# A selective-scan layer on one core: ScalarE's carry copy between the two halves of a step's exponentials

## The reference

```python
dA  = exp(dt_t[:, :, None] * A)                       # A = -exp(A_log), (512, 64)
hst = hst * dA + (dt_t * x_t)[:, :, None] * B_t[:, None, :]
y_t = einsum('bds,bs->bd', hst, C_t)                  # for every t, in order
```

## Time and profile before

| what | value |
|---|---|
| time, median of 3 runs | 5366.41 us (5361.21 to 5369.36) |
| the profiled execution | 5370.79 us |
| its span, first to last instruction | 5369.1 us |
| TensorE, VectorE busy | 93%, 88% of the span |
| GpSimd, ScalarE busy | 70%, 64% |
| mean granted TensorE clock | 0.987 of full speed |

### The profile page before, as it was taken

The page is one execution under the profiler, slowest core; times in us unless marked ns, Lnnn a source line. Parts: engine busy times, 40 slices in busy tenths (PEclk is TensorE's granted clock), DMA queues, the critical chain, the costliest instruction groups (busy, mean ns, idle before and its releaser), DMA issues. The chain is left out here.

```text
span 5369.1 us, 130492 instructions
## 1 busy us (share of the span) xinstructions
PE 4970.5 (93%) x44784; PEld 2522.5 (47%) x44784; DVE 4726.2 (88%) x2419; ACT 3415.8 (64%) x11498; POOL 3751.7 (70%) x6613
## 2 busy tenths in 40 slices
PE   6999999999999999999999999999999999886898
PEld 4444444444444444444444444444444444443444
DVE  2999999999999999999999999999999999996443
ACT  4666766666666766666676766666676766663112
POOL 4777768677777868777776868677776868674211
PEclk8999999999999999999999999999999999998899
DMA  3121111111121111112121111111121211113441
GB/s 106 38 64 43 54 48 52 54 39 61 38 64 42 55 48 52 55 38 61 38 64 43 61 41 52 55 37 61 39 63 39 64 38 43 36 29 104 146 153 66
DMA packets 433144, 306.75 MB, mean 57 GB/s; under 512 B 215920, under 2 KB 336240, under 8 KB 432496
## 3 DMA queue, kind: packets, MB, share of 16 engines
q1 hardware_dynamic: 428272, 294.39, 18.2%
q10 hardware_dynamic: 4224, 4.19, 0.2%
HBM read 187.27 MB, written 111.15 MB: 56 GB/s over the span
## 5 line engine op out<-in xcount | busy, mean ns | idle before, releaser
L891 DVE TENSOR_TENSOR_SCAN b_hs<-b_dA,b_u 128x1024 f32<-128x1024 f32 x2048 | 4540.7, 2270 | 273.9 <-ACT b_u L818 187.0
L1056 PE MATMUL b_ex<-b_dd,b_aw 32*128 32x512 f32 x8192 | 2710.1, 642 | 33.7 <-POOL b_dd L534 15.4
L1043 PE MATMUL b_u<-b_ud,b_bw 32*128 32x256 f32 x16384 | 2336.5, 401 | 258.9 <-DVE b_hs L891 237.6
L800 ACT ACTIVATE b_dA<-b_ex 128x496 f32<-128x496 f32 x4096 | 2289.7, 589 | 145.4 <-PE b_ex L1056 142.6
L1043 PEld LDWEIGHTS b_u<-b_ud,b_bw 32*128 32x128 f32 x16384 | 1425.9, 184 | 1119.1 <-issue 635.5
L1075 PE MATMUL b_y<-b_hs,b_cw 128*32 128x256 f32 x16384 | 1309.9, 390 | 2.3 <-DVE b_hs L891 2.3
L818 ACT ACTIVATE b_u<-b_hin 128x32 f32<-128x32 f32 x1792 | 364.7, 203 | 1192.2 <-PE b_u L1043 1006.9
L534 POOL TENSOR_TENSOR b_dd<-b_dr,b_mask 128x512 f32<-128x512 f32 x1024 | 1073.2, 1048 | 52.2 <-DVE b_hs L891 39.4
L543 POOL TENSOR_TENSOR b_ud<-b_ur,b_mask 128x512 f32<-128x512 f32 x1024 | 1083.5, 1058 | 0.0
L1056 PEld LDWEIGHTS b_ex<-b_dd,b_aw 32*128 32x128 f32 x8192 | 856.6, 183 | 106.7 <-ACT b_dA L800 65.9
L570 POOL TENSOR_TENSOR b_hm<-b_first,b_hs 128x32 f32<-128x32 f32 x1792 | 480.1, 268 | 539.4 <-ACT b_first L799 517.8
(11 more groups left out here) (104 smaller groups left out, 2283.1 us busy)
## 6 DMA issues: line engine op xcount, KB each, us to landing
b_u<-scratch_ut SPq DMA_DIRECT2D x256, 128.0 KB, 2.9
scratch_y<-b_ysb SPq DMA_DIRECT2D x128, 256.0 KB, 2.3
scratch_xs<-b_xs SPq DMA_DIRECT2D x64, 256.0 KB, 2.4
scratch_sz<-b_sd SPq DMA_DIRECT2D x64, 256.0 KB, 2.2
scratch_dt<-b_sd SPq DMA_DIRECT2D x64, 256.0 KB, 2.1
scratch_ut<-b_uT SPq DMA_DIRECT2D x64, 256.0 KB, 2.4
b_ur<-scratch_ut SPq DMA_DIRECT2D x1024, 16.0 KB
b_dr<-scratch_dt SPq DMA_DIRECT2D x1024, 16.0 KB, 1.7
```

The source lines that it names most:

```text
L800: nc.scalar.activation(dA[:, j % NDA, h, :, 1:TC], src[:, :, 1:TC], ACT.Exp).then_inc(exp_done, 1)
L891: nc.vector.tensor_tensor_scan(hs[:, v, :, :, kp].rearrange("p d t -> p (d t)"), dA[:, j % NDA, :, :, :].rearrange("p h d t -> p (h d t)") ...
L1043: ins = nc.tensor.matmul(dst[:, :, tb, :], bw[row(r), c % 2, tb, :], ud[row(r), j // 2 % NPR, tb, :, :], start=(tb == 0), stop=(tb == NTB ...
L1056: nc.tensor.matmul(e[bank_of[what]][:, :], aw[row(r), p % DIRS, v, :, :].rearrange("p b s -> p (b s)"), dd[row(r), (p * PAIRS + j // 2) % ...
```

## The change

In `one_pass` of ScalarE, the two halves of `decay` are called apart: half 0 of step j+2 ahead of `put_carry(p, j)`, half 1 behind it. `decay` gets the half as an argument; its waits for `scanned` and `hin_made` go with half 0, the wait for `e_done` stays with each half. The order in ScalarE's queue was carry copy, L799 and L800 of half 0, L799 and L800 of half 1; it becomes L799 and L800 of half 0, carry copy, L799 and L800 of half 1. Nothing is changed on the other engines.

```diff
-                def decay(p, j):
+                def decay(p, j, h):
                     c, k, kp, v = place(j)
-                    act.wait_ge(scanned, scanned_to(p, j - NDA))
+                    if h == 0:
+                        act.wait_ge(scanned, scanned_to(p, j - NDA))
+                        if c:
+                            act.wait_ge(hin_made, hin_to(p, j - NM))
+                    src = e[bank_of["e", 2 * (p * JP + j) + h]][:, :].rearrange("p (d t) -> p d t", t=TC)
+                    act.wait_ge(e_done[2 * (1 - kp) + h], p * (JP // 2) + (j // 2 + 1))
                     if c:
-                        act.wait_ge(hin_made, hin_to(p, j - NM))
-                    for h in range(2):
-                        src = e[bank_of["e", 2 * (p * JP + j) + h]][:, :].rearrange("p (d t) -> p d t", t=TC)
-                        act.wait_ge(e_done[2 * (1 - kp) + h], p * (JP // 2) + (j // 2 + 1))
-                        if c:
-                            nc.scalar.activation(e0[:, j % NM, h, :], src[:, :, 0], ACT.Exp).then_inc(e0_done, 1)
-                        nc.scalar.activation(dA[:, j % NDA, h, :, 1:TC], src[:, :, 1:TC], ACT.Exp).then_inc(exp_done, 1)
+                        nc.scalar.activation(e0[:, j % NM, h, :], src[:, :, 0], ACT.Exp).then_inc(e0_done, 1)
+                    nc.scalar.activation(dA[:, j % NDA, h, :, 1:TC], src[:, :, 1:TC], ACT.Exp).then_inc(exp_done, 1)
...
                     for j in range(JP):
                         half = (p * JP + j) // HALF
+                        then = (p, j + 2) if j + 2 < JP else None if last else (p + 1, j + 2 - JP)
+                        if then:
+                            decay(*then, 0)
                         if j >= STEPS:
                             put_carry(p, j)
-                        if j + 2 < JP:
-                            decay(p, j + 2)
-                        elif not last:
-                            decay(p + 1, j + 2 - JP)
+                        if then:
+                            decay(*then, 1)
...
-                decay(0, 0)
-                decay(0, 1)
+                for j in range(2):
+                    for h in range(2):
+                        decay(0, j, h)
```

## The result

| kernel | median, us | runs | ratio to before, 95% |
|---|---|---|---|
| before | 5366.5 (5361.2 to 5369.4) | 4 | |
| changed | 5484.4 (5481.1 to 5492.0) | 4 | 1.0223 [1.0205, 1.0241] |

A forecast was written before the change was run, and what follows sets the result against it. It took VectorE's scans (busy 4726.2 of 5369.1 us) and their loop through injection and carry copy as the bound; 140 us for back-to-back steps plus 10 for steps with a gap gave +150, 5516 us, range 5440 to 5600.

The forecast's parts named there:

- The pair: ScalarE's L799 and L800 of half 0, moved ahead of the carry copy; L799 forecast 1.25 us after the first injection.
- It holds the engine 0.54: On ScalarE the moved L799 and L800 delay the carry copy from 1.34 to 1.79 us after the first injection.
- Slack 0.27: In quiet even steps the carry copy could come 0.27 us later for nothing; a 0.45 delay makes the loop the bound.
- The loaded steps: Steps of passes with projections and transposes on TensorE; those without a gap pay the quiet price, 485 gaps judged apart.
- quiet price: Cost per step in the last pass, where only scan work runs: 0.107 us; for 1307 steps 140 us.
- +10: Net term in us for the 485 scans that start after a gap, taken between +109 and -55.
- first rival: Loaded passes swallow most: half their quiet steps hide behind TensorE, stalled steps at zero; +76 us, 5442, chance 0.15.
- second rival: Every loaded step pays in full, those with a gap too: 140 + 109 = +249 us, 5615, chance 0.13.
- Absorbed: Third rival: the carry copy's delay stays below 0.27 us, so the time stays at 5366 us, chance 0.06.
- faster: Fourth rival: TensorE gets its banks sooner and the carry's delay is hidden; -55 us, 5311, chance 0.05.
- fourth rival: First-half exponentials leave 0.22 us earlier, freeing TensorE's banks, with the carry's delay hidden: -55 us, 5311, chance 0.05.
- idle time of 0.18 us: Forecast sign in the last pass: VectorE idle about 0.18 us before every other scan, ended by the carry copy L818.

The follow-up runs named there:

- e4: Changed kernel, with TensorE's exponent matmul of half 0 of step j+2 issued ahead of its wait for scan j-2: 5428.7 us, ratio 1.0114.
- e1: Kernel before, with only the 16-column L799 of half 0 and its waits moved ahead of the carry copy: 5356.5 us, ratio 0.9981.
- e2: Kernel before, with L799 and 248 of the 496 columns of half 0 ahead of the carry copy: 5424.7 us, ratio 1.0109.
- e3: Kernel before, with all four ACTIVATEs of step j+2, both halves, ahead of the carry copy: 5808.6 us, ratio 1.0823.
- e6: Changed kernel, with the bank of half 0 reported free only with that of half 1: 5618.1 us, ratio 1.0464.
- e9: Kernel before, with the bank of half 0 reported free only with that of half 1: 5632.3 us, ratio 1.0496.

## Why the prediction was right, and where it was off

- *The pair can start only 0.09 us ahead of where the copy stood, at 1.25.* Right: 1.25. The counter-test is e4: with the exponent earlier, the same order is free in quiet steps.
- *It holds the engine 0.54.* Right: 4781.94 - 4781.39 = 0.55, the copy at 1.80 against 1.79. The copy behind an L800 stood in no trace yet; it was well read from an L799 in the same place.
- *Slack 0.27, then the loop is the bound.* Right: 4.57 us for two steps, +12.0 in the last pass, both as forecast. e1 and e2 stay below the slack, the changed kernel and e3 lie above it, and each last pass comes out within 1 us of its forecast: 0.0, 1.0, 12.0 and 42.4.
- *The loaded steps.* Mis-sized. I had 1307 steps at the quiet price, 12 of those 140 us in the last pass, and +10 for the 485 with a gap: 138 in loaded passes. They paid 106.5. The scans' starts of both traces, compared step by step, tell which term was off. In the loaded passes 1220 steps with a carry had no gap of 0.15 us or more before the change (30 of my 485 gaps stand before steps that have no carry); they took 119.2 us more, 0.098 each against my 0.107. The 460 with a gap took 12.2 us less. So the price of the back-to-back steps was nearly right, and the term that failed is the +10: it is -12. That is near the first rival's "stalled steps at zero"; its other half, that half of the back-to-back steps hide, was wrong, and so was its total of 76. e3, at twice the delay, has the same pattern: 383.6 us in the 1220, +13.3 in the 460. The split is by where the time appears: a delay in one step can shorten the gap of the next, so hiding behind TensorE's work shows up in the steps with a gap too. Whether the -12 is such hiding or the earlier banks isn't separated by any run.
- *Every loaded step in full (second rival).* Wrong: 5615 was forecast. *Absorbed, faster.* Wrong as said: L799 starts at 1.25. Yet with the size of e1, where the copy stays inside its slack, there is a small gain of 10 us. The fourth rival's mechanism may be behind it, since the large ACTIVATEs start 0.04 earlier, but that isn't shown.
- *What the profile would show.* VectorE's waits for L818 were to rise to about 320 us; the table has 270.9, without the idle times under 0.15 us. The idle time of 0.18 us before every other scan was mis-sized: in the last pass the records have 0.10 to 0.11 us before 55 of the 128 scans, 5.8 us in all.
- The Trainium skill (Perfetto Trace Analysis, Identifying the Most-Contended Engine) says to optimise the engine of the highest occupancy first. That a reordering on ScalarE, 64% busy, would therefore leave the time where it is was my reading and isn't what the page says. The reading failed: the run is 2.2% slower, through a loop that occupancy doesn't show.

## What to carry to other kernels

Idle time of an engine ahead of an instruction can be filled for nothing only by work whose inputs come early enough for it to end within that idle time and the slack behind it; ask what makes the filler ready, and put its time beside the end of the wait. On an engine that works through its queue in order, as ScalarE did here (copy at 1.36, 1.59, 1.80 and 2.32 us with more and more ahead of it), what goes ahead of a short link in a loop is paid once the loop's slack (here 0.27 us) is gone. Read slack and hold from start to start in the quietest stretch; there the price was forecast to within 1 us. In stretches where other engines set part of the pace, steps that start back to back paid nearly the quiet price and steps that had a gap already paid next to nothing, so count the two apart. But the slack of the quiet steps is no promise for loaded ones (e2), and two prices on different loops did not add (e6, e9).

## What was not expected

The three banks leave little room: reporting one of two banks a step free 0.5 us later costs 262 us (4.9%), more than twice what the late carry costs, though TensorE's own waits for L800 made only some 110 us in the profile before.
